# A perceiver block on one core: five waits at stage edges moved or taken away, and each value block of the cross attention handled in two halves at other places

## The reference

```python
# cross attention: 8 batches, 64 queries, 1601 context rows + 64 new ones each
q     = x_norm @ wq.T
k_new = x_norm @ wk.T
v_new = x_norm @ wv.T
k = concat([context, k_new]);  v = concat([context, v_new])
out = softmax(q @ k.T / 32) @ v
x = x + out @ wo.T
# then self attention with rotary positions and a causal mask over 64 tokens:
x = x + attn(layernorm(x))
# then 8 experts, each silu(x Wg) * (x Wu) @ Wd, weighted per token by a router:
x = x + ffn(layernorm(x))
```

## Time and profile before

| | us |
|---|---|
| median of 3 runs | 1279.72 |
| lowest, highest | 1274.67, 1285.12 |
| the profiled execution, its own time | 1284.38 |
| its span in the trace | 1282.6 |
| PE busy in it | 1211.0 (94%) |
| DVE, ACT, POOL busy | 819.6, 633.5, 95.7 |
| first unit of the attention starts on PE | 111.16 |
| its last matmul ends | 435.2 |

### The profile page before, as it was taken

The page is one execution under the profiler, slowest core; times in us unless marked ns, Lnnn a source line. Parts: engine busy times, 40 slices in busy tenths (PEclk is TensorE's granted clock), DMA queues, the critical chain, the costliest instruction groups (busy, mean ns, idle before and its releaser), DMA issues.

```text
span 1282.6 us, 19314 instructions
## 1 busy us (share of the span) xinstructions
PE 1211.0 (94%) x7810; PEld 1059.3 (83%) x7810; DVE 819.6 (64%) x1026; ACT 633.5 (49%) x604; POOL 95.7 (7%) x74
## 2 busy tenths in 40 slices
PE   5999999999989999999997699999999999999996
PEld 5887777777768888888886698989898999989894
DVE  7335789999997557463565473746565655646464
ACT  4114888888896423123543335344454444454440
POOL 0010000000000000000000012111121111111202
PEclk9999899999998999999999699999999999999998
DMA  7355799999998434220244276666667667666632
GB/s 290 139 164 191 290 338 363 370 374 363 372 392 321 190 114 164 99 99 34 100 143 163 89 245 185 226 205 212 213 211 216 209 220 212 215 197 224 195 132 33
DMA packets 46872, 272.98 MB, mean 213 GB/s; under 512 B 5880, under 2 KB 6024, under 8 KB 18528
## 3 DMA queue, kind: packets, MB, share of 16 engines
q1 hardware_dynamic: 36768, 243.48, 52.3%
q0 software_dynamic: 10048, 28.71, 9.2%
HBM read 255.92 MB, written 16.25 MB: 212 GB/s over the span
## 4 chain that ended last, share of the span: by engine, by line
PE 76%; DVE 9%; ACT 6%; issue 4%; DMA 3%; POOLq 0%; POOL 0%; SPq 0%; ACTq 0%; DVEq 0%
PE ps L1425 20%; PE ps L1426 20%; PE ps L1427 20%; PE ps L1538 6%; DVE lo L938 4%; ACT hi L628 3%; DMA out<-y,target 2%; PE ps L1651 2%; PE ps L1902 1%; PE ps L1586 1%; DVE stats L942 1%; ACT scores L696 1%; DMA raw<-weights 1%; PE ps L1744 1%; PE ps L1728 1%
## 5 line engine op out<-in xcount | busy, mean ns | idle before, releaser
L938 DVE TENSOR_TENSOR lo<-raw,hi 128x2048 fp32r<-128x2048 f32 (+1 forms) x198 | 443.7, 2251 | 168.3 <-ACT hi L628 165.8
L628 ACT ACTIVATE hi<-raw 128x2048 fp32r<-128x2048 f32 (+1 forms) x198 | 370.5, 1881 | 258.3 <-PE ps L1427 248.2
L1425 PE MATMUL ps<-act_hi,hi 128*128 128x240 f32 (+2 forms) x1232 | 362.0, 294 | 10.0 <-DVE h_lo L1394 4.2
L1427 PE MATMUL ps<-act_hi,lo 128*128 128x240 f32 (+2 forms) x1232 | 363.0, 295 | 0.0
L1426 PE MATMUL ps<-act_hi,hi 128*128 128x240 f32 x1024 | 284.4, 278 | 0.0
L1425 PEld LDWEIGHTS ps<-act_hi,hi 128*128 128x128 f32 x1232 | 235.6, 191 | 19.5 <-issue 7.3
L1427 PEld LDWEIGHTS ps<-act_hi,lo 128*128 128x128 f32 x1232 | 236.1, 192 | 6.9
L1426 PEld LDWEIGHTS ps<-act_hi,hi 128*128 128x128 f32 x1024 | 195.1, 191 | 0.3
L1425 PE MATMUL ps<-hi,act_hi 128*128 128x512 f32 x320 | 126.2, 395 | 0.0
L1427 PE MATMUL ps<-hi,act_lo 128*128 128x512 f32 x320 | 124.7, 390 | 0.0
L1426 PE MATMUL ps<-lo,act_hi 128*128 128x512 f32 x320 | 124.6, 389 | 0.0
(11 more groups left out here) (228 smaller groups left out, 1442.9 us busy)
## 6 DMA issues: line engine op xcount, KB each, us to landing
raw<-weights SPq DMA_DIRECT2D x124, 1024.0 KB, 4.9
raw<-keys SPq DMA_DIRECT2D x36, 1024.0 KB, 5.4
raw<-context SPq DMA_DIRECT2D x31, 1024.0 KB, 7.5
raw_more<-context SPq DMA_DIRECT2D x17, 1024.0 KB
raw_more<-keys SPq DMA_DIRECT2D x12, 1024.0 KB
xq<-x_in SPq DMA_DIRECT2D x4, 512.0 KB, 7.0
raw_more<-weights SPq DMA_DIRECT2D x4, 512.0 KB
new_keys_t<-kvs POOLq DMA_DIRECT2D x8, 256.0 KB, 3.5
```

The costliest lines, as they stand in the source:

```text
L628: act.activation(part(hi, k, kind), part(raw, k, kind), ACT.Copy).then_inc(hi_done, 1)
L938: dve.tensor_tensor(part(lo, k, kind), part(raw, k, kind), part(hi, k, kind), ALU.subtract).then_inc(lo_done, 1)
L1425: pe.matmul(out, a_hi, b_hi, start=first, stop=False)
L1427: return pe.matmul(out, a_lo, b_hi, start=False, stop=last)
```

## The change

1. `attention_units`: each value block becomes two units of 128 x 512 (256 KB), one behind each of two given units: behind K2 and K4 for batches 0 and 1, behind V1 and V3 for batches 0 to 5. The blocks of batches 2 to 6 so move from the keys to the values. The first half holds matmuls for four of the eight chunks of the sum, the second the other four.
2. `q_hi` of batches 0 and 1 moves from behind the last projection unit to behind the sixth, `q_lo` to behind the seventh, with the small setup of `twice` and `late_p` ahead of the whole loop.
3. For batch 0 `new_v_copy` stands ahead of `exps`, no longer behind the split that follows it.
4. `late(4)` moves from behind V4 of batch 6 to behind its V6.
5. An expert's first product waits for `xg_done` in four steps, one per two chunks, no longer for all four at once.
6. For the last expert POOL issues three of the four scatters ahead of reading `meta`.

```diff
-    def stretch(what, b, extra):
+    def stretch(what, b, places):
+        f = next(blocks) if places else None
         for u in range(7):
             yield what, b, u
-            if u == (4 if what == "keys" else 2) and extra:
-                yield "block", None, next(blocks)
-
-    units = list(stretch("keys", 0, True))
+            if u in places:
+                yield "block", places.index(u), f
+
+    units = list(stretch("keys", 0, (2, 4)))
     for s in range(B):
         if s + 1 < B:
-            units += stretch("keys", s + 1, s < 6)
-        units += stretch("values", s, s == 0)
+            units += stretch("keys", s + 1, (2, 4) if s == 0 else ())
+        units += stretch("values", s, (1, 3) if s < 6 else ())
...
-HALVES = {("keys", 7, 3): 0, ("keys", 7, 5): 1, ("values", 6, 0): 2, ("values", 6, 2): 3, ("values", 6, 4): 4,
+HALVES = {("keys", 7, 3): 0, ("keys", 7, 5): 1, ("values", 6, 0): 2, ("values", 6, 2): 3, ("values", 6, 6): 4,
           ("values", 7, 1): 5}
...
-            def load_block(k, f):
-                load(k, w_d[W_V + f // 2, :, (f % 2) * D:(f % 2 + 1) * D], dst=raw_of(k)[:, 0:D])
+            def load_block(k, f, h):
+                at = (f % 2) * D + h * HALF
+                load(k, w_d[W_V + f // 2, :, at:at + HALF], dst=raw_of(k)[:, 0:HALF])
...
             gather(0)
             for e in range(NE):
                 if e + 1 < NE:
                     gather(e + 1)
-                else:
-                    pool.wait_ge(meta_ready, 1)
-                    more = pool.value_load(meta[0:1, 0:1], min_val=0, max_val=MORE)
-                scatter(e)
+                    scatter(e)
+            scatter(NE - 1, ((0, 0), (0, 1), (1, 0)))
+            pool.wait_ge(meta_ready, 1)
+            more = pool.value_load(meta[0:1, 0:1], min_val=0, max_val=MORE)
+            scatter(NE - 1, ((1, 1),))
...
-                    if n > 0 and ATTENTION[n - 1][0] == "block":
+                    if n > 0 and ATTENTION[n - 1][0:2] == ("block", 1):
                         block_copy(ATTENTION[n - 1][2])
...
                             score_rows(b, 3)
                             if b == 0:
+                                new_v_copy(copied)
+                                copied += 1
                                 exps(0)
...
-            act.wait_ge(evacuated, O_QK + C)
-            q_hi(0)
-            q_hi(1)
+            for k in range(U_Q, U_KEYS0):
+                split(k + AHEAD)
+                if k == U_KEYS0 - 3:
+                    act.wait_ge(evacuated, O_QK + C)
+                    q_hi(0)
+                    q_hi(1)
...
-            def value_block(f, k):
-
-                if f == 0:
+            def value_block(f, h, k):
+
+                if h == 0 and f == 0:
                     pe.wait_ge(evacuated, O_QK + 16)
-                else:
+                elif h == 0:
                     pe.wait_ge(block_copied, f)
                 unit_ready(k)
-                for c in range(C):
-                    at = slice(c * P, (c + 1) * P)
+                for c in range(4 * h, 4 * h + 4):
+                    at = slice((c - 4 * h) * P, (c - 4 * h + 1) * P)
                     ins = three(ps[:, BLOCK_BANK, :], hi[:, k % RING, at], lo[:, k % RING, at],
                                 act_hi[:, c, :], act_lo[:, c, :], c == 0, c == C - 1)
-                ins.then_inc(block_ready, 1)
+                ins.then_inc(block_ready if h == 1 else unit_used, 1)
...
-                pe.wait_ge(xg_done, 4 * e + 4)
...
+                            if f == 0 and j == 0 and c % 2 == 0:
+                                pe.wait_ge(xg_done, 4 * e + (c // 2 + 1))
```

More of the change, by code:

```diff
@@ L125, in released @@
         if what == "block":
-            unit("block_ready", u + 1)
+            unit(*(("block_ready", u + 1) if b == 1 else (None, 0)))
         elif what == "keys":
@@ L467, in _ @@
                 else:
-                    load_block(U_KEYS0 + n, u)
+                    load_block(U_KEYS0 + n, u, b)
             for k in range(RING):
@@ L523, in gather, with scatter @@
                         .then_inc(gathered[n], 16)
[L525 to L535 removed]
+            def scatter(e, parts=((0, 0), (0, 1), (1, 0), (1, 1))):
+                for g, n in parts:
+                    pool.wait_ge(y_done, 4 * e + (2 * g + n + 2))
+                    pool.sem_inc(pool_passed, 1)
+                    pool.wait_ge(scattered, 16)
+                    pool.indirect_dma_start(out_d.rearrange("t (g d) -> (t g) d", g=2),
+                                            bass.IndirectOffsetOnAxis(ap=target[0:R, g, n:n + 1], axis=0),
+                                            y[0:R, n, g * HALF:(g + 1) * HALF], None, compute_op=ALU.add)\
+                        .then_inc(scattered, 16)
             gather(0)
@@ L579, in part @@
             if kind == BLOCK:
-                return whole[:, 0:D]
+                return whole[:, 0:HALF]
             return whole
@@ L586, in blocks_before @@
         def blocks_before(n):
-            return sum(what == "block" for what, _, _ in ATTENTION[:n])
+            return sum(what == "block" and h == 1 for what, h, _ in ATTENTION[:n])
         def tail_parts(buf, k):
@@ L672, in _ @@
             act.activation(wr_hi[:, :, :], wr_raw[:, :, :], ACT.Copy).then_inc(wr_hi_done, 1)
-            for k in range(U_Q, U_KEYS0):
-                split(k + AHEAD)
             def q_hi(s):
@@ L986, in _ @@
             dve.tensor_tensor(wr_lo[:, :, :], wr_raw[:, :, :], wr_hi[:, :, :], ALU.subtract).then_inc(wr_split, 1)
-            for k in range(U_Q, U_KEYS0):
-                split(k + AHEAD)
-                for j in range(2):
-                    f = 2 * k + j
-                    dve.wait_ge(out_ready, O_QK + f + 1)
-                    if f < C:
-                        dve.tensor_copy(q[:, 0:B, f, :], ps[:, f % 4, :].rearrange("p (b n) -> p b n", b=B))\
-                           .then_inc(evacuated, 1)
-                    else:
-                        if f >= C + 2:
-                            dve.wait_ge(kv_stored[f % 2], 16 * ((f - C) // 2))
-                        dve.tensor_copy(kvs[:, f % 2, :], ps[:, f % 4, :]).then_inc(evacuated, 1)
             def q_lo(s):
@@ L1078, in _ @@
             dve.memset(late_p[:, :, :], 0.0).then_inc(late_p_cleared, 1)
-            q_lo(0)
-            q_lo(1)
+            for k in range(U_Q, U_KEYS0):
+                split(k + AHEAD)
+                for j in range(2):
+                    f = 2 * k + j
+                    dve.wait_ge(out_ready, O_QK + f + 1)
+                    if f < C:
+                        dve.tensor_copy(q[:, 0:B, f, :], ps[:, f % 4, :].rearrange("p (b n) -> p b n", b=B))\
+                           .then_inc(evacuated, 1)
+                    else:
+                        if f >= C + 2:
+                            dve.wait_ge(kv_stored[f % 2], 16 * ((f - C) // 2))
+                        dve.tensor_copy(kvs[:, f % 2, :], ps[:, f % 4, :]).then_inc(evacuated, 1)
+                if k == U_KEYS0 - 2:
+                    q_lo(0)
+                    q_lo(1)
             attention()
@@ L1663, in attention @@
                     if what == "block":
-                        value_block(u, k)
+                        value_block(u, b, k)
                     elif what == "keys":
```

11 lines of the change are left out of this document (removed).

## The result

The changed kernel takes **1265.86 us** (median of 4 executions, 1263.64 to 1266.69) against 1279.1 (1274.67 to 1285.12) for the kernel before beside it: a ratio of 0.9891, 95% interval 0.986 to 0.9921, 13.2 us faster. The forecast was 1254, 26 us faster. The direction was right, the time lies in the range, and only half of the gain came. The time lies near the upper end of the range, and the largest part of what put it there, the load of the first weight, is in none of the rivals.

A forecast was written before the change was run, and what follows sets the result against it. PE is busy 94% of the span, so only its idle time and half-clock time can be won. Terms sum to 26.3 us off the profiled 1284.38, giving 1258.1; less 4.7 to the median, 1253.4, stated as 1254, range 1245 to 1268.

The forecast's parts named there:

- the eight added loads: SP's extra loads of the same bytes: costed at nothing; by the skill's fixed part alone 16 us, 1270 instead of 1254.
- q, 4.1: Start of K0, batch 0: splitting q early removes a 2.5 us wait and 1.6 us of low clock.
- new_v, 5.2: End of batch 0's keys: copy ahead of exponentials saves a 2.6 us wait and 3.4 of clock, less a new 0.8 wait.
- rival D: At batch 0's new_v, nothing won: the half block's new wait exceeds 1.8 us and the clock falls; 1260, chance 0.07.
- late(4), 8.5: Ahead of turn_o(6): late(4) fills the wait, 1.8 us won, plus 6.7 us of low clock behind it.
- Rival A: At batch 7 the clock falls all the same, so late(4) gives 1.8 instead of 8.5: 1261, chance 0.12.
- its sign: A fall of the clock near 405 would show the prediction wrong.
- The blocks among the values, 5.0: Five equal attention periods: halves among the values shorten each from 37.68 to 36.7 us, 5.0 in all.
- rival B: Periods stay at 37.7, set by DVE and ACT or the loads: 5 us less, 1259, chance 0.12.
- Rival C: One long V0 wait per period, clock falling at 1.6 to 1.8 us: 1267 (chance 0.06) to 1293 (slower, 0.03).
- xg_done, 1.2: Ahead of expert 0: waiting in four steps wins 0.8 to 1.5 us of a 1.5 us wait, taken as 1.2.
- the scatters, 2.3: End of the kernel: only POOL's last scatter stands behind meta, saving 2.3 us, between 1.9 and 2.8.

The follow-up runs named there:

- e5: Half blocks and shifted raw places kept, all five edges back as in the kernel before: 1275.45 us, ratio 0.9968.
- e4: The changed kernel's edges alone, with the old whole blocks at their old places (120 units): 1265.21 us, ratio 0.9877.
- e1: The changed kernel with each attention unit's raw place shifted four further on: 1256.45 us, ratio 0.981.
- e8: As e1, but q is split at its old place, behind the last key unit of the projection: 1262.78 us, ratio 0.9864.
- e9: As e1, but the copies of new_v stand behind the exponentials of batch 0 again: 1256.08 us, ratio 0.9813.
- e10: As e4 (whole blocks), but the copies of new_v stand behind the exponentials of batch 0 again: 1264.39 us, ratio 0.9871.
- e7: As e1, but late unit 4 stays behind V4 instead of V6: 1264.17 us, ratio 0.9882.
- e6: As e1, but one whole block behind V2 for batches 1 to 5, places shifted by 3 instead of 4: 1267.71 us, ratio 0.9909.
- e2: The changed kernel with the last score copy and its addition moved from K6 to V0 for batches 1 to 7: 1265.12 us, ratio 0.9882.
- e3: e2 with the shifted raw places of e1: 1256.61 us, ratio 0.9816.
- e12: As e1, but GpSimd reads the count ahead of all four last scatters, and an expert's first product waits once for all of xg_done: 1265.79 us, ratio 0.9896.
- e11: e3 with late units 1 to 3 one unit later: 1257.62 us, ratio 0.9824.

## Why the prediction was right, and where it was wrong

Put together, the medians:

| | old blocks | half blocks, places shifted |
|---|---|---|
| edges as before | 1279.4 | 1275.45 (e5) |
| edges of the change | 1265.21 (e4) | 1256.45 (e1) |

The half blocks with their places bring 4.0 us with the edges as before and 8.8 with the edges of the change, and the 4.8 between the two were not explained. The profiled executions can't show it: those of e4 and e1 lie 2.8 below and 5.4 above their medians, and their spans are almost equal (1260.6 and 1260.0). What follows therefore rests on single waits and stretches where it names traces, and on medians where it says so.

**Not in the sum: the place of the first weight.** The largest miss, 5.8 us by the trace of the change and 9.4 by medians (e1). The prediction costed the eight added loads at nothing because no load is late within the list. That nearly holds: ACT's waits for landings in the five periods add up to 1.8 us, where the kernel before has none. (Its sentence that ACT never waits for a landing overlooks one of 1.2 us at 10.04, ahead of the attention.) The step that failed is its limit to the list. Eight units more are one turn of the six places and two units over: place 0 goes from the sixth-last unit to the second-last, and the load that suffers is the first one behind the list, where PE had finished 16 us sooner than before and needed it sooner. With the places as they were, the forecast of 1254 would have been 2.5 us off, in part by luck: what `new_v` was to give by its order came from the half block, the periods gave less than forecast, and q and the scatters gave more.

The Trainium skill ("DMA: Bandwidth & Descriptors", "Anatomy of one DMA") gives each DMA a fixed part of about 2.0 us next to its bytes. By that part alone, with each of the eight loads in the path, the loss would have been 16 us, an estimate. No such loss shows: e1 has all eight and takes 1256.45, 8.8 us less than e4, which has none of them. The load that did stand in the path cost by the time of its issue, 413.47, with 5.6 us to its landing.

**q, 4.1.** Right in its kind and, by the medians, too small: 3.8 by the traces at `turn_o(1)`, 6.3 by medians (e8). The wait and the low clock behind it came and went with the edit.

**new_v, 5.2: a gain booked on the wrong edit.** The gain exists, but the copy's new order has no part in it (e9, e10). The prediction said "PE waited for it alone". It did not: with whole blocks DVE's `lo` of a later unit was late by nearly as much behind the same exponentials, and e4 shows it as soon as `new_v` is early: 2.7 for 2.6. What removes the long wait is the half block, which gives PE 2.8 us of work ahead of `turn_weights` and needs only 0.6 and 0.7 us of splits. The new wait there was forecast at 0.8 us and measured at 1.50, and the clock stayed up behind it. So rival D, which had it over 1.8 with a fall of the clock, was wrong as well.

**late(4), 8.5.** Right: 7.7 by medians, 7.4 by the traces (e7), of which some 1.8 are the shorter wait and the rest mostly the clock, 13.65 us at half speed. PE's wait for `kvs` is 0.35 us where 0.3 was forecast. Rival A, that the clock is down for 14 us all the same, is refuted in all eleven kernels with the new order; the short matmuls of `turn_o(6)` run at full clock. A shorter fall did come near 405, as its sign had it: 3.4 us behind a wait of 0.93 us ahead of V0, in nine of the eleven, though not in the changed kernel. It costs 1.7 us and was in no term.

**The blocks among the values, 5.0.** The mechanism was right, the size was not. Periods at full clock take about 37.0, not 36.7: 0.7 less than before, 3.5 in five. e6 shows that without the halves the new place brings nothing. Two links of the chain were missing. First, the chain goes from DVE's split of V1 straight to PE; in the trace it goes by ACT's copy of the last scores at K6, which waits for DVE's addition, and so to the split of V2. The pause is 3.6 us long, but it puts only 0.3 to 0.4 us a period into the chain; with half of it away (e2, e3) the periods come to 36.6 on average. Second, the short waits of ACT for landings. In e7, the one kernel of this order whose five periods have none, the four at full clock average 36.75, which is the forecast; the 38.25 of e9 has two such waits of 0.7 us. That is read from traces and was not tried. It is a part of rival B (periods at 37.7, with the loads as one of its reasons), whose number came true in the changed kernel: 188.09 for the five, though by the falls of the clock as well. The other part of the miss is the clock. In the trace of the change it fell in two of five periods (PEclk 0.96), at 1.7 us each, and that leaves 0.55 of 5.0. In e1, e7 and e8 it fell in one, in e9 and e12 in none, in e5 in three. Rival C had this at a wait of 1.6 to 1.8 us; it came behind waits of 1.06 to 1.26 at V0, and not behind all of them. Its lower price per fall, 1.7, was right, its condition was wrong. That two falls belong to the change and are not chance was not shown.

**xg_done, 1.2, and the scatters, 2.3.** The wait of 1.54 is gone, and e12 has 1.9 us for it at the place where it stands. The scatters gave 3.1 between the profiled executions and 3.5 in e12. Both were somewhat low. The medians of e12 say 9.3 for the two, and that is open.

**The level.** The forecast took the sum from the profiled execution and a further 4.7 us for its distance to the median. That execution of the kernel before lay 5.3 us above the median that was measured beside the change, the one of the change 0.8 above its own; this is the whole difference between 17.7 us gained in the profiled executions and 13.2 in the medians. A likely reason, not shown: the profiled execution before had a mean granted clock of 0.975, the others mostly 0.978 to 0.982, so part of its excess is time at low clock, the very thing that the sum removes, and is then counted twice. Which falls the others lacked no trace tells. Measured in the traces the sum was 8.6 too high: 4.5 for the periods, 5.8 for the first weight and 1.0 at batch 0, less 2.7 at other places, where the experts gave 3.6 more than forecast (the clock was down for 17.1 us at their start, before for 23.9, and the fall of 3.4 us at 805 is gone), the end gave 0.8 more, the end of batch 6 gave 1.4 less and the stretch up to the experts 0.3 less.

## What to carry to other kernels

Where buffers are dealt out by a counter, adding units to a list changes which buffer is free at its end: look at the last owner of the first buffer that the next stage takes, above all when the change also brings PE there sooner. A wait named after one thing may hide a second that is late by as much; list everything that is wanted at that point with its own time, and credit the gain only if all of it is earlier. And when edits come together, take each away alone from the whole: here one of them (`new_v`) was worth nothing, and one counter was worth as much as the largest edge. What the edits are worth alone need not add up to what they are worth together, and here 4.8 us of that stayed unexplained.

## What the runs showed of the hardware

The granted clock goes down to 1.2 GHz behind some of PE's waits, or in their last third of a microsecond, and not behind others of the same length. The wait of about a microsecond at V0 came five times in each of ten kernels with half blocks in the periods, and the clock fell behind 11 of these 50, for 3.4 us each time. The waits with a fall were 1.06 to 1.26 us long, those without one up to 1.23. In the changed kernel 1.13 and 1.25 us were followed by low clock, 1.22 and 1.13 us in the periods between were not. The wait of 1.50 at 134.32 was not, in any of the eleven kernels that have it.

Nor does a longer wait decide it. Ahead of `late`, waits of 1.87 to 1.97 us for `act_lo` were followed by a fall in e2, e3, e5, e7, e8 and e12 and not in the change, e1 and e9, and one of 2.77 us in e11 was not either. A wait of only 0.93 us ahead of V0 of batch 7, behind the short matmuls of `turn_weights`, was followed by one in nine of eleven kernels.

The wait of 2.14 us ahead of `turn_o(6)` brought some 14 us at half clock in the kernel before, in e5 and in e7. With 0.35 us in its place the PEclk of the 14 us behind it is 0.88 in e1 (the fall behind the 0.93 us, 6 us later) and 1.00 in the changed kernel.

Executions of one kernel differ along with the mean granted clock: 0.989 and 1258.88 us, 0.984 and 1266.83 us in e4. By these rows a wait of about a microsecond is not free: at V0 it was a chance of one in five to lose 1.7 us more.
